# Second attention closes its heads earlier; the plain feed-forward's first three chunks are prepared while it drains, its last chunk leaves in halves

## What is computed

```
x = x + gated_attention(norm(x), ctx)          # layer 0: 16 heads of 8, two layer norms, a gate
x = x + ffn0(norm(x))                          # 128 -> 512 -> 512 -> 512 -> 128, silu and gelu
x = x + attention(norm(x), ctx)                # layer 1: heads = softmax(q k / sqrt(8)) v ; heads @ w_o.T + b_o
x = x + relu(norm(x) @ W1 + b1) @ W2 + b2      # layer 1: 128 -> 512 -> 128, "plain feed-forward"
```

## Time and profile before

| | us |
|---|---|
| median of three runs | 972.93 |
| lowest, highest | 972.12, 976.82 |
| the profiled execution's own time | 975.65 |
| its span (first to last event) | 973.7 |
| PE, PEld busy | 932.2, 721.5 |
| DVE, ACT, POOL busy | 701.6, 785.3, 356.1 |

### The profile page before, as it was taken

How to read it: one execution, slowest core, us unless ns; L and a number is a source line. 1 busy time by engine, 2 the same in 40 slices (tenths; PEclk the granted TensorE clock), 3 DMA queues, 4 the chain that set the end, 5 groups by cost and what they waited for, 6 DMA issues and landing times.

```text
span 973.7 us, 33065 instructions
## 1 busy us (share of the span) xinstructions
PE 932.2 (96%) x12363; PEld 721.5 (74%) x12363; DVE 701.6 (72%) x1918; ACT 785.3 (81%) x1541; POOL 356.1 (37%) x543
## 2 busy tenths in 40 slices
PE   6999999999989999999999999899999999989997
PEld 3678778777668888878888887557777777658886
DVE  7789998887776766667667665366676765479985
ACT  7688888888778888888888887478888887758985
POOL 5889999997420000000000000254444442011110
PEclk9999999999999999999999999899999999999999
DMA  6333322211000000000000000022222221000111
GB/s 211 92 96 107 97 82 77 72 39 40 6 0 1 1 0 0 0 0 0 0 0 0 0 0 23 33 77 80 65 69 66 65 70 49 18 1 33 43 44 55
DMA packets 46548, 41.72 MB, mean 43 GB/s; under 512 B 24400, under 2 KB 32592, under 8 KB 46416
## 3 DMA queue, kind: packets, MB, share of 16 engines
q1 hardware_dynamic: 45216, 36.99, 12.4%
q10 hardware_dynamic: 1200, 2.90, 0.8%
HBM read 16.79 MB, written 4.19 MB: 22 GB/s over the span
## 4 chain that ended last, share of the span: by engine, by line
PE 79%; ACT 9%; issue 5%; DVE 4%; DMA 1%; ACTq 0%; SPq 0%; POOL 0%; DVEq 0%; POOLq 0%
PE ps_w L1070 15%; PE ps_w L1069 15%; PE ps_av L594 6%; PE ps_w L544 5%; ACT prob_t L692 4%; PE ps_w L541 3%; PE ps_mid L616 3%; PE ps_w L527 3%; PE ps_mid L617 3%; PE ps_turn L604 2%; ACT v_by_head L769 2%; PE ps_turn L631 2%; PE ps_mid L659 2%; PE p_ps_out L1068 2%; PE p_ps_out L1070 2%
## 5 line engine op out<-in xcount | busy, mean ns | idle before, releaser
L872 DVE TENSOR_REDUCE top<-ps_w 128x16 f32<-128x1024 f32 x128 | 155.9, 1218 | 78.9 <-PE ps_w L541 77.8
L1069 PE MATMUL ps_w<-g_h_lo,w_hi 128*128 128x512 f32 x512 | 206.2, 403 | 1.7 <-DVE g_h_lo L1304 1.7
L1070 PE MATMUL ps_w<-g_h_hi,w_hi 128*128 128x512 f32 x512 | 202.9, 396 | 0.0
L1304 DVE TENSOR_TENSOR g_h_lo<-g_h,g_h_hi 128x512 fp32r<-128x512 f32 x192 | 132.5, 690 | 87.3 <-ACT g_h_hi L1247 83.4
L133 POOL TENSOR_TENSOR front_rstd<-front_spread,minus_half 128x4 f32<-128x4 f32 x33 | 34.9, 1057 | 395.3 <-DVE front_spread L126 395.3
L541 PE MATMUL ps_w<-qk_sets,qk_t 32*64 32x256 f32 x2048 | 141.6, 387 | 0.1
L1247 ACT ACTIVATE g_h_hi<-g_h 128x512 fp32r<-128x512 f32 x192 | 121.3, 632 | 18.6 <-DVE g_h L1314 14.4
L692 ACT ACTIVATE prob_t<-ps_w 128x1024 f32<-128x1024 f32 x128 | 130.6, 1020 | 4.1 <-PE ps_w L544 4.0
L544 PE MATMUL ps_w<-qk_sets,qk_t 32*64 32x256 f32 x2048 | 132.6, 374 | 0.0
L1069 PEld LDWEIGHTS ps_w<-g_h_lo,w_hi 128*128 128x128 f32 x512 | 96.5, 189 | 25.2 <-DVE g_h_lo L1304 3.5
L1070 PEld LDWEIGHTS ps_w<-g_h_hi,w_hi 128*128 128x128 f32 x512 | 96.8, 189 | 21.4
(11 more groups left out here) (159 smaller groups left out, 2100.1 us busy)
## 6 DMA issues: line engine op xcount, KB each, us to landing
qk_sets<-qk_t SPq DMA_DIRECT2D x252, 64.0 KB, 1.9
ctx_in<-in_ctx SPq DMA_DIRECT2D x32, 128.0 KB, 2.9
ctx_in<-in_ctx_t SPq DMA_DIRECT2D x32, 128.0 KB, 2.4
out_x<-x_res SPq DMA_DIRECT2D x16, 256.0 KB, 2.0
x_res<-in_x SPq DMA_DIRECT2D x14, 256.0 KB, 3.2
shift<-pieces SPq DMA_DIRECT2D x128, 16.0 KB, 2.3
w_raw<-in_ff_weights SPq DMA_DIRECT2D x8, 256.0 KB, 3.2
w_raw<-in_ff_weights ACTq DMA_DIRECT2D x1, 768.0 KB, 8.5
```

The lines of the kernel that those rows point to most:

```text
L872: nc.vector.tensor_reduce(out=top[:, i % 2, half, :], in_=bank_pair(half).rearrange("p (a q) -> p a q", q=SEQ), op=ALU.max, axis=AX.X).the ...
L1069: nc.tensor.matmul(out, w_hi, x_lo, start=first and w_lo is None, stop=False)
L1070: return nc.tensor.matmul(out, w_hi, x_hi, start=False, stop=last)
L1304: nc.vector.tensor_tensor(h_lo[level][:, o, :], h[:, o % 2, :], h_hi[level][:, o, :].bitcast(F32), ALU.subtract).then_inc(lo_ready[level], 1)
```

## The change

Three edits, all in layer 1's part:

- DVE's order in a step of attention 1: rden now stands ahead of rest, and heads_out directly behind rest, ahead of the residual sum. Layer 0 keeps its order.
- The drain prepares more. In step N DVE measures chunks 0 and 1, in N+1 it normalises both; POOL takes both powers in N. PE transposes chunk 1 directly behind chunk 0 in step N+2, into bank 3 of ps_w, and the bridge's two matmuls in N+3 are gone for this layer. ACT copies chunk 1 in step N+3, DVE takes its remainder there, and W1's output 3 of chunk 0, which overwrites bank 3, waits for it. DVE measures chunk 2 in N+2 and normalises it in N+4. The feed-forward's own steps begin to prepare with chunk 3. W2 of chunk 0 waits quarter by quarter.
- The end: chunk 14 is turned back between the second and third quarter of chunk 15's W2. Chunk 15's bias, turn back (into `ps_back` and `ps_turn`), sum and store are done in two halves of 256 rows.

```diff
-def front_turn_in(nc, t, front, pe, i, s, bank):
+def front_turn_in(nc, t, front, pe, i, s, bank, own_bank=False):
     pe.wait_ge(front.norm_ready, i + 1)
-    wait(pe, front.x_lo_ready, i)
+    if not own_bank:
+        wait(pe, front.x_lo_ready, i)
...
-    BRIDGE = {N + 2: 4, N + 3: 2}
+    BRIDGE = {N + 2: 4, N + 3: 2} if gated else {N + 2: 4}
...                                              # PE, first_products
                 for o in outputs:
+                    if o == 3:
+                        pe.wait_ge(front.x_lo_ready, 2)
...                                              # PE, step
                     front_turn_in(nc, t, front, pe, 0, 0, ps_w[:, 0:CHUNK])
+                if not gated and j == N + 2:
+                    front_turn_in(nc, t, front, pe, 1, 1, ps_w[:, 3 * CHUNK:4 * CHUNK], own_bank=True)
...
-                if not gated and j == N + 4:
-                    front_turn_in(nc, t, front, pe, 1, 1, ps_turn[:, :])
...                                              # ACT
-                if not gated and j == N + 4:
-                    front_take_in(nc, t, front, act, 1, 1, ps_turn[:, :])
+                if not gated and j == N + 3:
+                    front_take_in(nc, t, front, act, 1, 1, ps_w[:, 3 * CHUNK:4 * CHUNK])
...                                              # POOL
                 if j == N:
-                    front_power(nc, t, front, pool, 0, 0)
+                    for n in range(1 if gated else 2):
+                        front_power(nc, t, front, pool, n, n)
                 if j == N + 2:
-                    front_power(nc, t, front, pool, 1, front.slots - 1)
+                    front_power(nc, t, front, pool, 1 if gated else 2, 0)
...                                              # DVE; invert_sums is rden, close_heads is heads_out
+                if not gated:
+                    invert_sums(j - 3)
                 i = j
                 if on(i):
                     dve.wait_ge(top_split, 6 * i + 3)
                     ...                          # rest
+                if gated:
+                    invert_sums(j - 3)
+                else:
+                    close_heads(j - 3)
                 ...                              # residual sum of unit j - 4
+                if gated:
+                    close_heads(j - 3)
                 ...                              # pieces
                 if j == N:
-                    wait(dve, x_done if gated else y_taken, 2)
-                    front_measure(nc, t, front, dve, 0, 0)
-                    front_moments(nc, t, front, dve, 0, 0)
-                    front_spread(nc, t, front, dve, 0, 0)
+                    wait(dve, x_done if gated else y_taken, 2 if gated else 4)
+                    for n in range(1 if gated else 2):
+                        front_measure(nc, t, front, dve, n, n)
+                        front_moments(nc, t, front, dve, n, n)
+                        front_spread(nc, t, front, dve, n, n)
                 if j == N + 1:
-                    front_normalise(nc, t, front, dve, 0, 0)
+                    for n in range(1 if gated else 2):
+                        front_normalise(nc, t, front, dve, n, n)
...
                 if j == N + 2:
                     front_split_in(nc, t, front, dve, 0, 0, ps_w[:, 0:CHUNK])
-                    wait(dve, x_done if gated else y_taken, 4)
-                    front_measure(nc, t, front, dve, 1, front.slots - 1)
+                    following = 1 if gated else 2
+                    wait(dve, x_done if gated else y_taken, 2 * following + 2)
+                    front_measure(nc, t, front, dve, following, 0)
                     ...                          # moments and spread alike
                 if not gated and j == N + 3:
-                    front_normalise(nc, t, front, dve, 1, front.slots - 1)
+                    front_split_in(nc, t, front, dve, 1, 1, ps_w[:, 3 * CHUNK:4 * CHUNK])
                 if not gated and j == N + 4:
-                    front_split_in(nc, t, front, dve, 1, 1, ps_turn[:, :])
+                    front_normalise(nc, t, front, dve, 2, 0)
...                                              # plain feed-forward: measured(i) is i > 2, final(i) is i == N - 1
+            def turn_back(i, s):
+                ...                              # not final: as before
+                for n in range(2):
+                    pe.wait_ge(out_taken, i + 1 + n)
+                    if n == 0:
+                        pe.wait_ge(x_done, i)
+                    for k in (2 * n, 2 * n + 1):
+                        last = nc.tensor.transpose(last_half(n)[:, k % 2 * P:(k % 2 + 1) * P], out_t[:, s, k * P:(k + 1) * P], t.ident[:, :])
+                    last.then_inc(back_done, 1)
...
-                    wait(pe, lo_ready, 4 * i + 4)
+                    opening = isinstance(i, int) and i == 0
+                    if not opening:
+                        wait(pe, lo_ready, 4 * i + 4)
                     wait(pe, out_taken, i - 1)
                     for c in range(4):
+                        if opening:
+                            pe.wait_ge(lo_ready, c + 1)
+                        if final(i) and c == 2:
+                            turn_back(i - 1, u)
...                                              # ACT
-                    nc.scalar.activation(out_t[:, s, :], bank(ps_out, s), ACT.Identity, bias=t.b2[:, 0:1]).then_inc(out_taken, 1)
+                    for part in (slice(0, UNIT), slice(UNIT, CHUNK)) if final(i) else (slice(0, CHUNK),):
+                        nc.scalar.activation(out_t[:, s, part], bank(ps_out, s)[:, part], ACT.Identity, bias=t.b2[:, 0:1]).then_inc(out_taken, 1)
...                                              # POOL and DVE: ahead(j + 3) becomes measured(j + 3), ahead(j + 2) measured(j + 2)
+                if final(i):
+                    for n in range(2):
+                        rows = t.x[:, i * CHUNK + n * UNIT:i * CHUNK + (n + 1) * UNIT]
+                        dve.wait_ge(back_done, i + 1 + n)
+                        nc.vector.tensor_tensor(rows, last_half(n)[:, 0:UNIT], rows, ALU.add).then_inc(x_done, 1)
...                                              # SP
-            with sp.Fori(0, N) as i:
+            with sp.Fori(0, N - 1) as i:
                 ...
-            sp.wait_ge(stored, 16 * N)
+            for n in range(2):
+                half = slice((N - 1) * CHUNK + n * UNIT, (N - 1) * CHUNK + (n + 1) * UNIT)
+                sp.wait_ge(x_done, N + n)
+                sp.dma_start(t.out[:, half], t.x[:, half]).then_inc(stored, 16)
+            sp.wait_ge(stored, 16 * (N + 1))
```

More of the change, by code:

```diff
@@ L873, in highest, with invert_sums, close_heads @@
                                         op=ALU.max, axis=AX.X).then_inc(top_ready, 1)
+            sums = ps_av[:, :].rearrange("p (h r) -> p h r", r=PAIR_COLS)
+            def invert_sums(i):
+                if on(i):
+                    dve.wait_ge(sums_back, i + 1)
+                    nc.vector.reciprocal(rden[:, :, :], sums[:, :, PER_TILE * HEAD_DIM:PER_TILE * HEAD_DIM + PER_TILE]).then_inc(rden_ready, 1)
+            def close_heads(i):
+                if on(i):
+                    dve.wait_ge(rden_ready, i + 1)
+                    wait(dve, heads_t_done, i)
+                    nc.vector.tensor_tensor(heads_out[:, :, :].rearrange("p b (h d) -> p h b d", d=HEAD_DIM),
+                                            sums[:, :, 0:PER_TILE * HEAD_DIM].rearrange("p h (b d) -> p h b d", d=HEAD_DIM),
+                                            rden[:, :, :].unsqueeze(3).to_broadcast([P, HEADS, PER_TILE, HEAD_DIM]),
+                                            ALU.mult).then_inc(heads_ready, 1)
             def step(j):
@@ L1370, in ahead, with measured, final @@
         return on(i) and not (isinstance(i, int) and i <= 1)
+    def measured(i):
+        return on(i) and not (isinstance(i, int) and i <= 2)
+    def final(i):
+        return isinstance(i, int) and i == N - 1
     with ExitStack() as ctx:
@@ L1400, in plain_feed_forward, with last_half @@
         stored = sem("stored")
+        def last_half(n):
+            return (ps_back, ps_in)[n]
         def bank(of, n):
@@ L1405, in tensor_program @@
         def tensor_program(pe):
+            def turn_back(i, s):
+                if not on(i):
+                    return
+                if not final(i):
+                    pe.wait_ge(out_taken, i + 1)
+                    wait(pe, x_done, i)
+                    for k in range(CHUNK_TILES):
+                        last = nc.tensor.transpose(ps_back[:, k * P:(k + 1) * P], out_t[:, s, k * P:(k + 1) * P], t.ident[:, :])
+                    last.then_inc(back_done, 1)
+                    return
+                for n in range(2):
[4 more added lines that the diff above has]
+                        last = nc.tensor.transpose(last_half(n)[:, k % 2 * P:(k % 2 + 1) * P], out_t[:, s, k * P:(k + 1) * P], t.ident[:, :])
```

(20 more changed lines are left out.)

17 lines of the change are left out of this document (2 added, 15 removed).

## The result

| | before | after |
|---|---|---|
| median, us (runs) | 974.93 (13) | 970.55 (13) |
| lowest, highest | 972.06, 980.49 | 965.92, 971.92 |
| ratio, 95% interval | | 0.995 (0.9932 to 0.9968) |
| the profiled execution's own time, its span | 975.65, 973.7 | 971.22, 969.0 |

The change is faster by 4.4 us between the medians and by 4.9 (3.1 to 6.6) in the ratio, half a percent. Forecast was a saving of 5.55 from a base of 972.93, which is 967.3 with a range of 964.8 to 970.0; 970.55 lies above the range. Taken from 972.93, that range is a saving of 2.9 to 8.1: the measured saving is inside it, the absolute time is not. Beside the later kernels the kernel before had medians of 975.82 (23 runs), 976.27 (16) and 973.76 (19).

The account below looks back on a forecast made before the run. PE was taken to bound the kernel, busy 96% of the span. 6.4 us at the drain and feed-forward start plus 0.55 at the tail made 6.95; without the slow stretch 5.55, so 967.3 us from 972.93, range 964.8 to 970.0.

Parts of the forecast that it names:

- the second: Base for the whole time: median execution without the stretch at reduced clock, 972.93 - 5.55 = 967.4; the other choice gave 966.0.
- Part 2: Start of feed-forward: chunk 1's products at 860.4 instead of 863.51, chunk 2's at 867.6 instead of 874.02; 6.4 us, 5.0 at full clock.
- slow stretch: Chunk 0's twelve down products from 869.57, mostly at 1.2 GHz: 4.45 us against 2.90 at full clock, 1.55 more.
- The first and second rivals: Drain: DVE becomes late, 969.4, chance 0.15; first feed-forward products: the clock falls, 968.3, chance 0.15.
- Part 1 in the drain: Drain: heads_out ends at 842.18 instead of 842.73, so L594 and the chain behind it start earlier by 0.55 us.
- the bridge's 0.12: Drain: two bridge matmuls go (0.57), four transposes of chunk 1 take their place (about 0.44): 0.12 us gained.
- Part 1 in the steady steps: Attention 1: heads_out ends earlier, but L594 still waits for v_by_head, so 0 gained over 28 steps.
- One sign named for part 1: Attention 1: DVE's idle time ahead of rest (0.41 us) shrinks by the reciprocal, and rest starts no later.
- Part 3: Tail, last chunk in halves: x_done at 969.85 instead of 970.38; 0.55 us gained, between 0.2 and 0.9.
- Rival 4: Feed-forward's first steps take the head start back, ACT or DVE setting them; only 1.1 us remains: 971.8, chance 0.05.

Follow-up runs that it names:

- the drain alone: Only the early preparation of chunks 0 to 2 added to the kernel before, with its old DVE order and old tail: 970.67 us, ratio 0.993.
- drain and tail: Early preparation and the last chunk in halves added to the kernel before, with its old DVE order: 969.91 us, ratio 0.9958.
- the light: The changed kernel with attention 1's scatter of queries and keys cut to 64 bytes a row: 967.37 us, ratio 0.9906.
- the wide kernel: The changed kernel with probabilities times values in 16 matmuls of 128 columns a unit for 32 of 64: 960.91 us, ratio 0.9832.
- the wide kernels: 16 matmuls of 128 columns for 32 of 64 a unit, in the changed kernel (960.91 us) and in the kernel before (972.83 us).
- the two ratios: The whole change against the kernel before, in two series: 970.55 us, ratio 0.995, and once more 969.81 us, ratio 0.9946.
- the kernel with the step of 6.59: The kernel before with only heads_out moved ahead of the residual sum, the reciprocal left behind rest: 977.44 us, ratio 1.0018.

## Why the prediction came out as it did

**What failed.** The time lies 3.25 us above the forecast. The step that failed is the choice of the base: "I take the second, nearer to where the median stands below the profile", which took 972.93, a median of three runs, for the kernel before; 13 runs put it at 974.93, 2.0 higher. The other 1.2 are the saving, 4.4 for 5.55. The interval of the ratio holds 5.55, so that these 1.2 may be noise; but the traces show a term that the sum lacks and that can account for most of it: 0.7 to 1.0 between rest 61 and rest 63, where PE stalls in all three profiles with the whole order and all instructions, and in one of four with the old. Behind that is a second failed step, the reading of the earlier trace rows in part 1.

**Part 2, right to a few tenths.** Forecast: chunk 1's products at once, chunk 2's 10.1 us after the first products (867.6 less 857.5), and 14.42 for the old way at full clock. Measured: 9.95 to 10.15 in six profiles, and 14.44 to 14.64. So the gain is 4.4 here, 5.8 with a slow stretch in the old kernel. The wait that comes late next is the one named, chunk 2's x_lo (1.00 us for 1.15 forecast). The first and second rivals did not come: x_lo of chunk 1 was in time for all but 0.24 us of a weight load, and the clock stayed at 1.00 in the drain and at the new start in all six profiles that have them. The Trainium skill (TensorE: Matmul & The Clock Gate, Part 4: PE-mode transpose) says that a transpose does not count as busy PE in the way a matmul does, by which the clock would have fallen in the new drain. None of these profiles shows that: the eight transposes of the two chunks, with the bridge's four matmuls, stood ahead of the products and the clock did not fall.

**Part 1 in the drain: 0.45 for 0.67** (0.55 and the bridge's 0.12). In the three profiles with the whole order that compute everything it is 0.25 to 0.46, in the light and the wide kernel against theirs 0.64 and 0.73; the exchange of bridge for transposes gave nothing (16.25 and 16.26 with the drain alone and with drain and tail, 16.26 before). And the new order loses more just ahead of it: 0.7 to 1.0 between rest 61 and rest 63.

**Part 1 in the steady steps: the sum right by luck, its reason wrong.** Forecast was 0, because "L594 still waits for v_by_head". The step that failed is the reading of the earlier trace rows: the releaser named there was one that had been met long before, and heads_out closed the steps. The mechanism forecast would have left the step at 6.74; it fell to 6.48, which is 0.26 x 26 = 6.8 us of wait removed. Had I read that rightly and stopped, the forecast would have been 7 us too low: by the runs all of it, as far as the profiles can tell, comes back in steps that are long because PE stalls without waiting for another engine. Profiles of one program differ here by 1.2 (175.30 and 176.51); the wide kernels aside, with the old order the 26 steps took 175.08 to 176.48, with the new one 173.96 to 176.51. That it comes from the number of PE's instructions is shown by the wide kernels (7.0 us between 175.30 and 168.29, with 832 matmul instructions and as many weight loads fewer; with the old order the same cut gave 1.9 at most). That it is the fetch of blocks rests on the packets' count and on their times beside the 28 stalls; no run changes the fetch alone. Why it falls on those units, and whether the loop's branches have a part, stays open. One sign named for part 1 also failed: DVE's idle time ahead of `rest` did not shrink by the reciprocal (0.45 for 0.41).

**Part 3: 0.65 for 0.55** over six profiles on each side. Between the two profiles of before and after it is 0.31. The six of each side spread over 0.6.

**Rival 4, that the head start is taken back,** did not come: from chunk 2's products to chunk 15's first down product it is 90.62 before and 90.75 after, 6.5 a chunk as forecast, though the terms given for that (24 products at 0.24, eight transposes at 0.11) add up to 6.64.

**The sum.** 0.5 in the drain, 4.4 at full clock or 5.8, and 0.65 make 5.5 to 6.9, for 5.55 and 6.95 forecast; less the 0.7 to 1.0 between rest 61 and rest 63 it is 4.5 to 6.2. The medians have 4.4, the two ratios 4.9 and 5.3, with 3.1 to 7.4 in their intervals. Larger than what is left between these is the error of the base. I subtracted from 972.93, the median of three runs, and took its distance from the profiled execution as a sign that the median lacks the slow stretch. Four series of 13 to 23 runs (the first holds those three) put the kernel before at 973.76 to 976.27. Their mean of 975.2 less 5.55 is 969.6, and 974.93 less 5.55 is 969.4, 1.2 from what was measured. The three runs themselves spread over 4.7 us, and the range of 5.2 that I gave held the doubt on the steps, hardly that on the base.

## What to carry to other kernels

A releaser named in a wait must be matched by unit: check that the instance which ended last is the one that the wait is for, and compare the distance from the other candidate with one seen where it certainly released (0.26 us in a steady step, in the drain and in the kernel with the step of 6.59). A shorter step is only worth its difference if PE can be fed: count its instructions for each step, see whether idle time "issue" appears at fixed places as soon as the step is shorter, and lay the times of the instruction queue's packets beside it. With few runs of a kernel, the base is as uncertain as the change; give the range both.

## What the runs showed of the hardware

- In attention 1 about 314 PE instructions a step (8176 in 26) went through at 6.74 us a step mostly without a stall and, at 6.48, with stalls of up to 1.43 us, so that the mean came back to 6.74 to 6.79. At 250 a step, 6.46 held but for two of the 26 steps (6.71, 6.63).
- Each of 28 stalls of PE over 0.3 us with no releaser, in twelve profiles of attention 1, ended 1.2 to 1.7 us after the end of a 16 KB packet of the queue "q8 instruction". There is a packet for about 248 matmuls and weight loads.
- From the end of the VectorE instruction that releases it to the start of the matmul it was 0.26 us, three times.
- The start of the program up to the first `rest` takes 28.3 to 29.3 or 30.4 to 31.1 us, for the same program in different executions.
- At the old start of the feed-forward the granted clock was at 0.50 for a stretch in three profiles of six: in two over chunk 0's down products, where it cost 1.4 to 1.6 us (15.84 and 16.03 beside 14.44), in one over chunk 1's first products, with no cost that can be seen (14.44).
